# Mamba block and mixture of experts on one core: GpSimd's four softplus operations of batches 2 to 6 as one instruction of 1024 columns each

## What is computed

```python
xz = rms_norm(xn) * norm_w @ in_proj_w.T           # 2 x 256 channels: x_s and z
u = silu(causal_conv4(x_s) + conv_b)
dt, B, C = split(u @ x_proj_w.T)                   # 8, 16 and 16 columns
delta = softplus(dt @ dt_proj_w.T + dt_proj_b)     # the step size, 256 channels
h = exp(delta * A) * h + (delta * u) * B           # over 512 times, for each of 16 states
y = sum over states of h * C, + u * D
mamba = (y * silu(z)) @ out_proj_w.T + xn
moe = top 2 of 8 experts, gated, each silu(x @ w_gate) * (x @ w_up) @ w_down
```

## Time and profile before

| | before |
|---|---|
| median of 3 runs | 607.68 us (607.37 to 607.71) |
| the profiled execution's own time | 606.02 us |
| its span, first to last instruction | 604.2 us |
| VectorE busy | 581.3 us, 96% of the span |
| TensorE busy | 535.1 us, 89% |
| GpSimd busy | 489.8 us, 81%, 383 instructions |
| ScalarE busy | 465.9 us, 77% |

### The profile page before, as it was taken

How to read it: one execution, slowest core, us unless ns; L and a number is a source line. 1 busy time by engine, 2 the same in 40 slices (tenths; PEclk the granted TensorE clock), 3 DMA queues, 4 the chain that set the end, 5 groups by cost and what they waited for, 6 DMA issues and landing times.

```text
span 604.2 us, 11465 instructions
## 1 busy us (share of the span) xinstructions
PE 535.1 (89%) x3578; PEld 419.5 (69%) x3578; DVE 581.3 (96%) x841; ACT 465.9 (77%) x952; POOL 489.8 (81%) x383
## 2 busy tenths in 40 slices
PE   5899889898898998999989999899989697778887
PEld 2377766647787878877887778877777465656564
DVE  6999989989999999999999999999999998999997
ACT  3899696369957998579876798768995589969880
POOL 3793466479999899998999889998997967885784
PEclk9899798989999999999999999999999999989999
DMA  7320229625787887889768888778874455233374
GB/s 200 148 91 2 74 60 282 226 84 184 237 314 237 311 277 222 292 244 339 262 189 305 276 305 275 243 257 274 284 264 157 156 219 197 103 100 108 79 143 87
DMA packets 61038, 122.48 MB, mean 203 GB/s; under 512 B 8362, under 2 KB 41778, under 8 KB 53938
## 3 DMA queue, kind: packets, MB, share of 16 engines
q1 hardware_dynamic: 53826, 112.42, 55.1%
q0 software_dynamic: 6144, 9.00, 6.6%
q10 hardware_dynamic: 1008, 0.33, 0.3%
HBM read 112.25 MB, written 9.47 MB: 201 GB/s over the span
## 4 chain that ended last, share of the span: by engine, by line
POOL 34%; PE 26%; DVE 15%; issue 14%; ACT 10%; DMA 1%; ACTq 0%; DVEq 0%; POOLq 0%; SPq 0%
POOL dbu L996 18%; POOL xs L980 6%; DVE bank L1213 6%; DVE h_sb L1232 5%; PE bank L1507 4%; PE bank L1541 3%; PE bank L1672 3%; ACT dbu L570 3%; PE bank L1686 2%; PE bank L1556 2%; ACT da L542 2%; PE bank L1564 2%; PE bank L1680 2%; POOL delta L463 2%; POOL sp_m L448 2%
## 5 line engine op out<-in xcount | busy, mean ns | idle before, releaser
L996 POOL TENSOR_TENSOR dbu<-du,xn_all 128x1024 f32<-128x1024 f32 x86 | 203.6, 2368 | 22.3 <-DVE bank L1213 13.7
L1213 DVE TENSOR_TENSOR_SCAN bank<-bank,dbu 128x512 f32<-128x512 f32 x160 | 195.2, 1222 | 1.0 <-ACT bank L554 0.7
L1232 DVE TENSOR_TENSOR h_sb<-bank,xh_all 128x512 f32<-128x512 f32 x230 | 152.5, 677 | 1.0
L1507 PE MATMUL bank<-id_sb,h_sb 128*128 128x128 f32 x992 | 132.5, 277 | 11.8 <-DVE h_sb L1232 9.3
L554 ACT ACTIVATE bank<-delta,a_sb 128x512 f32<-128x512 f32 x170 | 117.1, 691 | 27.5 <-DVE h_sb L1232 22.8
L1507 PEld LDWEIGHTS bank<-id_sb,h_sb 128*128 128x128 f32 x992 | 112.5, 143 | 26.5 <-DVE h_sb L1232 14.5
L1213 DVE TENSOR_TENSOR_SCAN bank<-da,bank 128x512 f32<-128x512 f32 x82 | 96.1, 1213 | 4.0 <-PE bank L1468 3.2
L1672 PEld LDWEIGHTS bank<-wd_sb,hid 117*128 117x128 f32 (+1 forms) x432 | 55.4, 190 | 42.8 <-issue 26.3
L980 POOL DMA_INDIRECT xs<-xn_rows,src x72 | 70.4, 978 | 12.8 <-issue 9.5
L1672 PE MATMUL bank<-wd_sb,hid 117*128 117x128 f32 (+1 forms) x432 | 62.9, 281 | 17.9 <-ACT xT L769 17.9
L570 ACT ACTIVATE dbu<-du_t,bc_sb 128x256 f32<-128x256 f32 x164 | 69.4, 497 | 5.8 <-PE bank L1468 3.4
(11 more groups left out here) (205 smaller groups left out, 906.8 us busy)
## 6 DMA issues: line engine op xcount, KB each, us to landing
xh_all<-b_rows SPq DMA_DIRECT2D x30, 1024.0 KB
xn_all<-b_rows SPq DMA_DIRECT2D x25, 1024.0 KB
wgu_sb<-in_w_gu SPq DMA_DIRECT2D x72, 352.0 KB, 4.2
wd_sb<-in_w_dn SPq DMA_DIRECT2D x72, 192.0 KB, 5.8
y_slots<-ys SPq DMA_DIRECT2D x72, 64.0 KB
xn_rows<-xn_all SPq DMA_DIRECT2D x2, 1040.0 KB, 10.2
out<-x_sb SPq DMA_DIRECT2D x7, 256.0 KB, 7.2
x_sb<-in_x SPq DMA_DIRECT2D x2, 640.0 KB, 5.9
```

Source lines behind the costliest of these rows:

```text
L996: nc.gpsimd.tensor_tensor(dbu[k % 2][:, :, :], du[b % 2][:, :, :], b_ring[c % 2][:, k % CH, :].unsqueeze(1).to_broadcast([P, NH, T]), ALU. ...
L1213: nc.vector.tensor_tensor_scan(to, da_of(n)[:, hf, :] if n in IN_SBUF else at, inp, 0.0, ALU.mult, ALU.add).then_inc(s["h_rdy"], 1)
L1232: nc.vector.tensor_tensor(h_sb[k % 2][:, hf, :], bank_of(b, 2 * k + hf)[:, :], row, ALU.mult).then_inc(s["p_rdy"], 1)
L1507: last = MM(HT[i][:, t % 2, hf * P:(hf + 1) * P], h_sb[k % 2][:, hf, t * P:(t + 1) * P], id_sb[:, :], is_transpose=True, start=(k == 0 and ...
```

## The change

front() of GpSimd calls a new function for batches 2 to 6, which are prepared in stages 1 to 5. It does each of the four operations once, on both halves (1024 columns), in the step in which the second half was done before: 5, 8, 11 and 13. Each raises its semaphore by 2. The waits are those of the second halves. Batches 1 and 7 are as before.

```diff
+            def wide_front(b, q, k):
+
+                if k == 5:
+                    pool.wait_ge(s["sp_exp"], 2 * b + 2)
+                    nc.gpsimd.tensor_tensor(sp_m[:, :, :], sp_m[:, :, :], sp_y[:, :, :], ALU.add).then_inc(s["sp_sum"], 2)
+                if k == 8:
+                    pool.wait_ge(s["sp_corr"], b)
+                    pool.wait_ge(s["sp_sum"], 2 * b + 2)
+                    nc.gpsimd.tensor_tensor(sp_m[:, :, :], sp_m[:, :, :], sp_e[:, :, :], ALU.subtract).then_inc(s["sp_rem"], 2)
+                if k == 11:
+                    pool.wait_ge(s["sp_ln"], b + 2)
+                    pool.wait_ge(s["da_rdy"], 2 * S * (b - 1))
+                    pool.wait_ge(s["sp_rem"], 2 * b + 2)
+                    nc.gpsimd.tensor_tensor(delta[q][:, :, :], sp_d[:, :, :], sp_m[:, :, :], ALU.add).then_inc(s["delta_rdy"], 2)
+                if k == 13:
+                    if b == 2:
+                        pool.wait_ge(s["dut_mm"], 2)
+                    pool.wait_ge(s["delta_rdy"], 2 * b + 2)
+                    nc.gpsimd.tensor_tensor(du[q][:, :, :], delta[q][:, :, :], u_sb[b % 3][:, :, :], ALU.mult).then_inc(s["du_rdy"], 2)
+
             def front(b, q, k):
+                if 1 < b < 7:
+                    wide_front(b, q, k)
+                    return
                 if k in RAISE_AT[b - 1]:
```

## The result

The change measured 608.5 us (606.89 to 610.17, 21 executions) against 606.87 us (605.18 to 608.29, 21) of the kernel before: a ratio of 1.0023 with a 95% interval from 1.0013 to 1.0032. That is slower by about 0.23%, where I had forecast no change; the time lies inside the range. The profiled execution took 608.51 us, its span is 606.4.

The account below looks back on a forecast made before the run. VectorE was taken as the bound, with GpSimd just fitting in stages 2 to 4. Only stage 1 had a term: 607.68 - 0.14 = 607.5 us, no change (chance 0.85); range 606.6 to 609.3 us.

Parts of the forecast that it names:

- The price of a wide instruction: On GpSimd: each 1024-column instruction takes 2.37 us, like L996; 3.8 us less busy time in the profile.
- Stages 2 to 4: GpSimd's last product comes 0.15 us late for VectorE's scan, absorbed by the 0.29 us gate wait; term: nothing.
- Stage 1: GpSimd's 0.14 us delay before VectorE's scan at 180.82 goes, since step 12 is bare; term: -0.14 us.
- The rival of the chain: Stages 1 to 4: GpSimd is the path, each wide instruction returns 0.13 us; 2.1 us faster, 605.6 us; chance 0.05.
- the term for stage 5 and what follows: Stage 5: products after the wide input scale come later but before their scans; term: nothing, 0.8 us to spare.
- feeds a tile four steps on: Gather issued behind a GpSimd product: at most 0.75 us later, its tile used four steps on; no term.
- the bound: Whole kernel: a measurement can tell about 0.2%, or 1.2 us, from no change.
- a dearer instruction: Rival, stages 1 to 4: wide instructions cost more than L996's row says; 2.5 us slower, 610.1 us; chance 0.10.

Follow-up runs that it names:

- e7: The kernel before without the correction of the sum (L448) for batches 2 to 6, 12 us less GpSimd work; ratio 1.0000 [0.9984, 1.0016].
- e8: The change with one more GpSimd instruction of 220 columns in step 13 of stages 1 to 4; ratio 1.0017 [0.9998, 1.0037].

## Why the prediction was wrong, point by point

- **The price of a wide instruction** was right: 2.37 us, 363 instructions. GpSimd's busy time is 487.2 us where I had 486. I had taken off 20 x 0.19, but the busy time counts the 0.05 us in which two instructions overlap only once, so it falls by the 0.13 of the path, 20 x 0.13 = 2.6. (An estimate from the Trainium skill, GPSIMD Engine Reference, section Performance versus the Vector engine, leaves 0.06 us saved for a pair; the rows give 2 x 1.28 less 2.37, so 0.19.)
- **Stages 2 to 4** were right to 0.1 us: the products' starts, the wait of 0.87, the last scan late by 0.08 (I had 0.15) and swallowed at the gate, and 72.32 us a stage. e7 and e8 show both sides of it: work taken from GpSimd brings nothing, half a microsecond more costs 0.23. One reading was wrong: VectorE is idle before nine instructions between 190 and 407 us, three on each of the three lines of the earlier trace rows, not seven; nothing hangs on it.
- **Stage 1.** The gap of 0.14 us before the scan at 180.82 is gone: VectorE's lag against before falls from 1.08 to 0.94 us at that scan, and the product for it, begun at 178.34, has 0.94 us to spare. After:

```profile
178.34 2.38 POOL L996 TENSOR_TENSOR dbu<-du,xn_all 128x1024 f32<-128x1024 f32 x1
...
181.76 1.22 DVE L1236 TENSOR_TENSOR_SCAN bank<-bank,dbu 128x512 f32<-128x512 f32 x1
```
But the term did not reach the end: at L1289 the lag is 1.02 again, at the late first scan of the next stage 1.09, and from the gate at 194.78 on it is 1.03 or 1.04, so 0.05 are left. Against the differences between executions that is nothing: stage 1 took 71.33 to 71.65 us in the five profiles of the change, and 71.60 and 71.73 in the two of the kernel before.
- **The rival of the chain** fell: GpSimd's 34% of the chain is no measure of what shortening it returns. With 12 us of its work left out (e7_less_work) the time stayed within 1 us, where the chain promised 9.8.
- **The step that failed is the term for stage 5 and what follows:** "Term: nothing, with 0.8 us to spare." The scans of stage 5 did have the room. The product of step 15 begins 0.86 us later than before once VectorE's 1.05 us are taken off (474.90 less 1.05 less 472.99; I had 0.8), and no scan waits for it. After, against the earlier trace rows:

```profile
470.16 2.37 POOL L996 TENSOR_TENSOR dbu<-du,xn_all 128x1024 f32<-128x1024 f32 x1
...
474.90 2.37 POOL L996 TENSOR_TENSOR dbu<-du,xn_all 128x1024 f32<-128x1024 f32 x1
```
But the 0.86 us go on past stage 5: GpSimd's gathers of stage 6 stand in the same queue and have no slack until the third, which takes up 0.28 of it, and the fourth, which takes up the rest. So the gathers of steps 1 and 2 slide together in front of TensorE's turn of step 3, and VectorE waits 0.5 to 0.6 us there for that turn. I had followed the lateness to the next scan and stopped; of the gathers I said only that one "feeds a tile four steps on", which is the loads' case, not theirs. Cost: 0.3 to 0.4 us in stage 6 by profiles, 0.45 ± 0.28 us by the executions of the later measurements, 0.65 with the first. Why gathers that stand close hold up the turn's signal stays open.
- **The second fault is the bound.** I took 0.2% as what a measurement can tell, and gave no row for it; the three executions that I had lay within 0.34 us. In 184 executions the kernel before ran from 603.72 to 609.48. The first measurement had 1.4 us between the means, more than twice what five together show. The convolution at the start alone goes with 2 us in some executions and none in others, so an uneven share of them can make most of that: in that measurement 13 of the 21 executions of the change lie above 608.2 us and 2 of the 21 of the kernel before, in all measurements 31 of 68 and 45 of 184. That the rest of this unevenness is chance is not shown. A cost of 0.1% is within my 0.2%, the first measurement's 0.23% is not. That its 608.5 us lies inside my range is luck: I had the room above for a dearer instruction, which did not come.

## What to carry to other kernels

Work moved later on an engine that is not the bound must be followed to the place where that engine is next idle (here the fourth gather of stage 6), not to the next consumer: its later instructions, DMA issues above all, arrive late as well, and can bunch up before another engine's work. Judge the room stage by stage from the starts of two engines side by side; the longest share in the chain said nothing here. And before a few tenths of a per cent are believed, compare the stages' lengths in the profile, where equal stages mostly agree to 0.02 us, and repeat the measurement, since the start of the program alone can move the total by 0.3%.

## What the runs showed of the hardware that I had not expected

- TensorE's first long run of matmuls takes 7.14 us or 8.8 to 9.2 us, with up to five of 16 at 0.85 us apart instead of 0.43, while the granted clock reads 1.00 there.
- The stretches at 1.2 GHz later on (mostly 3.4 us, some 6.8, three to nine of them in a profile) lie at other times from execution to execution. None fell between 130 and 480 us in any profile, and stages 2 to 4 repeat to 0.02 us but for four profiles with one longer stage each, by 0.24 to 1.5 us (and e8, where the work was added); stage 7 took 55.65 us where none fell into its first 10 us and 56.03 to 57.79 us in the eight profiles where one did.
- The four gathers back to back take 0.95 us each with 0.30 us between, and VectorE's scan waits 0.5 to 0.6 us longer for TensorE's turn with them. The wait shrinks to 0.25 us when the third gather starts 0.3 us earlier and is gone when it starts 0.4 us earlier: a coupling that no record of the trace explains.
